# Latent attention layer on one core: the probabilities are split into halves before they are turned, and two transposing DMAs per query tile turn them in place of TensorE

## The reference, cut to what matters

```python
q_c = hidden @ Wq_c.T + bq_c                    # 192 latent channels
q   = (q_c @ Wq_up.T + bq_up)                   # 32 heads x (128 + 64)
kv  = hidden @ Wkv_c.T + bkv_c                  # 64 latent + 64 shared rope channels
k_nope, v = split(kv[:, :64] @ Wkv_up.T + bkv_up)    # 32 heads x (128 + 128)
scores = einsum('bhqd,bhkd->bhqk', q, [k_nope, k_rope]) / sqrt(192)
attn   = softmax(scores)                        # 1024 x 1024 for each head and batch
o      = einsum('bhqk,bhkv->bhqv', attn, v)
out    = o @ Wo.T summed over the heads + bo     # Wo is 512 x 128
```

## Time and profile before

| | |
|---|---|
| median of 3 runs | 1908.35 us (1903.71 to 1908.86) |
| the profiled execution's own time | 1908.44 us |
| its span (first to last instruction) | 1906.4 us |
| mean granted TensorE clock | 0.996 of full speed |
| busy: PE, DVE, ACT, POOL | 1878.7, 1615.1, 1398.4, 1237.8 us |
| the loop over the 128 rounds | about from 95 to 1800 us |
| one round in the middle | 13.2 us |

### The profile page before, as it was taken

How to read it: one execution, slowest core, us unless ns; L and a number is a source line. 1 busy time by engine, 2 the same in 40 slices (tenths; PEclk the granted TensorE clock), 3 DMA queues, 4 the chain that set the end, 5 groups by cost and what they waited for, 6 DMA issues and landing times. The chain is left out here.

```text
span 1906.4 us, 31285 instructions
## 1 busy us (share of the span) xinstructions
PE 1878.7 (99%) x11028; PEld 1174.0 (62%) x11028; DVE 1615.1 (85%) x2600; ACT 1398.4 (73%) x2491; POOL 1237.8 (65%) x1356
## 2 busy tenths in 40 slices
PE   7899999999999999999999999999999999999999
PEld 6756666665666666666666666666666666666544
DVE  5678888888888888888888888888888888888775
ACT  5567777777777777777777777777777777777622
POOL 3346766777666777777767667676666766767620
PEclk9999999999999999999999999999999999999999
DMA  5522112121111111111111111111112211111201
GB/s 205 175 83 45 42 38 45 35 45 38 41 43 36 45 35 45 46 34 45 40 40 42 38 45 36 43 45 34 45 35 45 46 34 45 37 43 41 84 33 58
DMA packets 74421, 96.68 MB, mean 51 GB/s; under 512 B 25856, under 2 KB 48416, under 8 KB 74272
## 3 DMA queue, kind: packets, MB, share of 16 engines
q1 hardware_dynamic: 70176, 86.33, 17.4%
q0 software_dynamic: 4096, 8.40, 1.3%
HBM read 83.95 MB, written 10.75 MB: 50 GB/s over the span
## 5 line engine op out<-in xcount | busy, mean ns | idle before, releaser
L965 DVE TENSOR_TENSOR PTL<-X,PTH 128x512 f16<-128x512 f32 x1024 | 657.1, 683 | 146.7 <-ACT PTH L913 146.3
L913 ACT ACTIVATE PTH<-X 128x512 f16<-128x512 f32 x1024 | 554.3, 594 | 236.0 <-PE X L815 236.0
L982 DVE TENSOR_REDUCE mx<-S 128x1 f32<-128x1024 f32 x512 | 621.4, 1214 | 3.0 <-PE S L838 3.0
L931 ACT ACTIVATE prob<-S,shift,unscale 128x1024 f32<-128x1024 f32 x512 | 620.3, 1212 | 0.3 <-DVE shift L988 0.2
L815 PE MATMUL X<-ident,prob 128*128 128x128 f32 x4096 | 538.0, 274 | 5.1 <-ACT prob L931 3.7
L815 PEld LDWEIGHTS X<-ident,prob 128*128 128x128 f32 x4096 | 458.3, 140 | 131.0 <-ACT prob L931 91.6
L836 PE MATMUL S<-kvTH,qeH 128*128 128x512 f16 x1024 | 388.1, 379 | 0.0
L837 PE MATMUL S<-kvTL,qeH 128*128 128x512 f16 x1024 | 388.1, 379 | 0.0
L838 PE MATMUL S<-kvTH,qeL 128*128 128x512 f16 x1024 | 388.1, 379 | 0.0
L777 POOL TENSOR_TENSOR onormH<-osum,recip_row 128x512 fp32r<-128x512 f32 x127 | 194.7, 1533 | 283.3 <-ACT osum L940 283.3
L843 PE MATMUL O<-PTH,kvn 128*128 128x512 f16 x1024 | 262.7, 379 | 0.6 <-DVE qef L971 0.4
(11 more groups left out here) (256 smaller groups left out, 2022.2 us busy)
## 6 DMA issues: line engine op xcount, KB each, us to landing
recip_row<-row_scratch SPq DMA_DIRECT2D x128, 256.0 KB, 4.3
weff<-weff_scratch SPq DMA_DIRECT2D x128, 192.0 KB, 4.5
wv<-in_wv POOLq DMA_DIRECT2D x128, 64.0 KB, 2.7
raw<-in_raw SPq DMA_DIRECT2D x8, 772.0 KB, 6.6
weff_scratch<-w_split SPq DMA_DIRECT2D x8, 768.0 KB, 5.8
x<-in_x SPq DMA_DIRECT2D x4, 1024.0 KB, 6.9
x_all<-in_x SPq DMA_DIRECT2D x3, 1024.0 KB, 5.8
out<-y SPq DMA_DIRECT2D x3, 1024.0 KB, 4.3
```

Source lines behind the costliest of these rows:

```text
L913: nc.scalar.activation(PTH[p][:, part:part + 4, unit * P:(unit + 1) * P], X[:, k % 2, :].rearrange("p (k c) -> p k c", k=4), ACT.Copy).the ...
L931: nc.scalar.activation(prob[u][:], S[:, u % 2, :], ACT.Exp, bias=shift[:, col:col + 1], scale=keep["unscale"][:, 0:1], accum_out=rs[:, col ...
L965: v.tensor_tensor(PTL[p][at], X[:, k % 2, :].rearrange("p (k c) -> p k c", k=4), PTH[p][at], ALU.subtract).then_inc(low_out, 1)
L982: v.reduce_max(mx[:, col:col + 1], S[:, u % 2, :], AX.X).then_inc(max_ready, 1)
```

## The change

The probabilities are no longer turned by TensorE. The exponential writes fp32 back into the slot of `S` that it read. ACT then copies that slot, 1024 columns in one instruction, to the fp16 high part (`halves[u][:, 0, :]`), and DVE subtracts it from the slot to get the low part (`halves[u][:, 1, :]`), both still with queries on the partitions. SP turns each of the two with one transposing DMA from SBUF to SBUF, 128 by 1024 fp16, into `PT` (eight 128 by 128 blocks of the high part, and eight of the low part): the one of the high part after `high_out`, the one of the low part after `low_out`. `X` is gone and `S` has three slots; a slot is free when `low` has read it.

What else moves: the values' matmuls of a head run two rounds later and not one, in one piece behind `scores(0)` (`values`). ACT's copy of `O` to `osum` and the first exponential of a round stand behind them. ACT and no longer DVE makes `qef`; POOL makes both `qeH` (a new fp16 copy) and `qeL` (`split_q`). POOL no longer writes the stacked tiles `onormLH` and `wvHL`, and PE adds a head's output with three matmuls in place of two (`output`), at the end of the round. DVE's copy of `V` moves to head 2.

```diff
-        prob = [sb(f"prob{i}", [P, SEQ]) for i in range(UN)]
-        PTH = [sb(f"PTH{i}", [P, KEYT, BLK], F16) for i in range(2)]
-        PTL = [sb(f"PTL{i}", [P, KEYT, BLK], F16) for i in range(2)]
+        halves = [sb(f"halves{i}", [P, 2, SEQ], F16) for i in range(UN)]
+        PT = [sb(f"PT{i}", [P, 2 * KEYT, BLK], F16) for i in range(2)]
...
-        S = ctx.enter_context(nc.psum_tensor("S", [P, 2, SEQ], F32))
-        X = ctx.enter_context(nc.psum_tensor("X", [P, 2, BLK], F32))
+        S = ctx.enter_context(nc.psum_tensor("S", [P, SLOTS, SEQ], F32))
         O = ctx.enter_context(nc.psum_tensor("O", [P, BLK], F32))
         V = ctx.enter_context(nc.psum_tensor("V", [P, BLK], F32))
...
+            def turn(g, u, par):
+
+                cols = slice(u * P, (u + 1) * P)
+                sp.wait_ge(high_out, UN * g + u + 1)
+                sp.dma_start(PT[par][:, 0:KEYT, cols], halves[u][:, 0, :], transpose=True).then_inc(turned_high[u], 16)
+                sp.wait_ge(low_out, UN * g + u + 1)
+                sp.dma_start(PT[par][:, KEYT:2 * KEYT, cols], halves[u][:, 1, :], transpose=True).then_inc(turned_low[u], 16)
+
             def body(g, b, h, par):
+                last = 1 - par
                 if exists(g + 2):
                     load(g + 2, dram["weff_h"][(h + 2) % NH], par)
                 if exists(g - 1):
 
-                    last = 1 - par
-
                     sp.wait_ge(recip_ready, g)
                     sp.dma_start(dram["row"][last].rearrange("(p u) -> p u", u=UN),
                                  recip[:, last * UN:(last + 1) * UN]).then_inc(recip_out, 16)
+                if exists(g):
+                    if g >= 2:
+                        sp.wait_ge(pv_done, g - 1)
+                    turn(g, 0, par)
+                if exists(g - 1):
                     sp.wait_ge(recip_out, 16 * g)
                     sp.dma_start(recip_row[last][:], dram["row"][last].partition_broadcast(P)).then_inc(row_in[last], 16)
+                if exists(g):
+                    for u in range(1, UN):
+                        turn(g, u, par)
...
-            def low_q(nxt, i):
+            def split_q(nxt, i):
                 pool.wait_ge(q_copied, nxt + 1)
+                nc.gpsimd.tensor_copy(qeH[i][:], qef[i][:]).then_inc(q_high, 1)
+                pool.wait_ge(q_high, nxt + 1)
                 nc.gpsimd.tensor_tensor(qeL[i][:], qef[i][:], qeH[i][:], ALU.subtract).then_inc(q_low, 1)
...
-                    nc.gpsimd.tensor_tensor(wvs[:], wv[i][:], unit[:], ALU.mult).then_inc(copied, 1)
-                    nc.gpsimd.tensor_tensor(wvHL[i][0:KVL, :], wv[i][0:KVL, :], unit[0:KVL, :], ALU.mult)
+                    nc.gpsimd.tensor_tensor(wvs[:], wv[i][0:KVL, :], unit[0:KVL, :], ALU.mult).then_inc(copied, 1)
                     pool.wait_ge(copied, 2 * g)
-                    nc.gpsimd.tensor_tensor(wvHL[i][KVL:P, :], wvs[KVL:P, :], f32(wvH[i][KVL:P, :]),
-                                            ALU.subtract).then_inc(wv_split, 1)
+                    nc.gpsimd.tensor_tensor(wvL[i][:], wvs[:], f32(wvH[i][0:KVL, :]), ALU.subtract).then_inc(wv_split, 1)
...
-                    nc.gpsimd.tensor_tensor(turned(onormH[:]), turned(osum[:]), row, ALU.mult).then_inc(onorm_high, 1)
-                    nc.gpsimd.tensor_tensor(turned(onorm[0:KVL, :]), turned(osum[0:KVL, :]), row[0:KVL],
-                                            ALU.mult).then_inc(onorm_high, 1)
-                    pool.wait_ge(onorm_high, 2 * g - 2)
-                    nc.gpsimd.tensor_tensor(turned(onormLH[KVL:P, :]), turned(osum[0:KVL, :]), row[0:KVL],
+                    nc.gpsimd.tensor_tensor(in_order(onormH[:]), in_order(osum[:]), row, ALU.mult).then_inc(onorm_high, 1)
+                    nc.gpsimd.tensor_tensor(in_order(onorm[:]), in_order(osum[0:KVL, :]), row[0:KVL],
                                             ALU.mult).then_inc(onorm_ready, 1)
+                    pool.wait_ge(onorm_high, g - 1)
                     pool.wait_ge(onorm_ready, g - 1)
-                    nc.gpsimd.tensor_tensor(onormLH[0:KVL, :], onorm[0:KVL, :], f32(onormH[0:KVL, :]),
-                                            ALU.subtract).then_inc(onorm_low, 1)
+                    nc.gpsimd.tensor_tensor(onormL[:], onorm[:], f32(onormH[0:KVL, :]), ALU.subtract).then_inc(onorm_low, 1)
...
-            def transposes(g, k, unit):
-
-                if event(g, k) > 2:
-                    pe.wait_ge(low_out, event(g, k) - 2)
-                for j in range(4):
-                    tile = 4 * (k % 2) + j
-                    last = nc.tensor.transpose(X[:, k % 2, j * P:(j + 1) * P], prob[unit][:, tile * P:(tile + 1) * P], ident[:])
-                last.then_inc(x_filled, 1)
...
-                    if 4 * g + u >= 2:
-                        pe.wait_ge(probs_ready, 4 * g + u - 1)
+                    if t >= SLOTS:
+                        pe.wait_ge(low_out, t - SLOTS + 1)
...
+                def values():
+
+                    if on:
+                        pe.wait_ge(q_copied, g + 1)
+                    for u in range(UN):
+                        pe.wait_ge(turned_high[u], 16 * (g - 1))
+                    for kt in range(KEYT):
+                        mm(O[:], keep["kvn"][:, batch * KEYT + kt, :], PT[par][:, kt, :], start=(kt == 0), stop=False)
+                    for u in range(UN):
+                        pe.wait_ge(turned_low[u], 16 * (g - 1))
                     for kt in range(KEYT):
                         half = slice(kt % 2 * KVL, (kt % 2 + 1) * KVL)
-                        ins = mm(O[half, :], keep["kvn"][:, batch * KEYT + kt, 0:KVL], PTL[1 - par][:, kt, :],
-                                 start=False, stop=(kt >= KEYT - 2))
-                    ins.then_inc(pv_done, 1)
+                        last = mm(O[half, :], keep["kvn"][:, batch * KEYT + kt, 0:KVL], PT[par][:, KEYT + kt, :],
+                                  start=False, stop=(kt >= KEYT - 2))
+                    last.then_inc(pv_done, 1)
+
+                def output():
+                    pe.wait_ge(wv_split, g - 1)
+                    pe.wait_ge(onorm_high, g - 1)
+                    pe.wait_ge(onorm_low, g - 1)
+                    mm(V[:], wvH[par][:], onormH[:], start=False, stop=False)
+                    mm(V[:], wvH[par][0:KVL, :], onormL[:], start=False, stop=False)
+                    mm(V[:], wvL[par][:], onormH[0:KVL, :], start=False, stop=h == (1 if on else 0)).then_inc(wv_done, 1)
...
+                if on:
+                    scores(0)
...
+                if exists(g - 2):
+                    values()
+                if on:
+                    scores(1)
+                    if exists(g + 1):
                         next_queries()
...
+                    scores(2)
+                    scores(3)
...
+                if exists(g - 2) and exists(g - 1):
+                    output()
...
-            def high_q(nxt, h, i):
+            def copy_q(nxt, h, i):
                 act.wait_ge(q_filled, nxt + 1)
+                if nxt >= 2:
+                    act.wait_ge(q_low, nxt - 1)
                 bias, factor = keep["beff"][:, h:h + 1], keep["qscale"][:, 0:1]
-                nc.scalar.activation(qeH[i][:], O[:], ACT.Identity, bias=bias, scale=factor).then_inc(q_high, 1)
+                nc.scalar.activation(qef[i][:], O[:], ACT.Identity, bias=bias, scale=factor).then_inc(q_copied, 1)
...
+                def exp(u):
+                    t, col = UN * g + u, par * UN + u
+                    act.wait_ge(shift_ready, t + 1)
+                    nc.scalar.activation(S[:, t % SLOTS, :], S[:, t % SLOTS, :], ACT.Exp, bias=shift[:, col:col + 1],
                                          scale=keep["unscale"][:, 0:1],
                                          accum_out=rs[:, col:col + 1]).then_inc(probs_ready, 1)
...
+                def high(u):
+                    t = UN * g + u
+                    act.wait_ge(probs_ready, t + 1)
+                    if g:
+                        act.wait_ge(turned_high[u], 16 * g)
+                    nc.scalar.activation(halves[u][:, 0, :], S[:, t % SLOTS, :], ACT.Copy).then_inc(high_out, 1)
+
+                if exists(g - 2):
+                    if g >= 3:
+                        act.wait_ge(onorm_high, g - 2)
+                        act.wait_ge(onorm_ready, g - 2)
+                    act.wait_ge(pv_done, g - 1)
+                    nc.scalar.activation(osum[:], O[:], ACT.Copy).then_inc(o_out, 1)
+                if exists(g):
+                    for u in range(UN):
+                        if u == 2 and exists(g + 1):
+                            copy_q(g + 1, (h + 1) % NH, 1 - par)
+                        exp(u)
+                        high(u)
...
+            def low(t):
+                u = t % UN
+                dve.wait_ge(high_out, t + 1)
+                if t >= UN:
+                    dve.wait_ge(turned_low[u], 16 * (t // UN))
```

(6 more changed lines are left out.)

216 lines of the change are left out of this document (73 added, 143 removed).

## The result

The changed kernel takes 2011.7 us (median of 4 runs, 2007.2 to 2014.6) against 1908.5 us: 1.0545 times the time, with a 95% interval of 1.0518 to 1.0571. It is 5.5% slower; 2080 us was forecast, 9%.

A forecast was written before the change was run, and what follows sets the result against it. SP's queue was taken to bound the round: 8 x (0.32 + 1.36) plus 1.07 for plain DMAs, 14.5 us. 1908.4 + 127 x (14.5 - 13.17) + 2 = 2080 us; 8-in-10 range 1845 to 2750.

The forecast's parts named there:

- What bounds before, and PE's work: PE sets the 13.17 us round; without transposes (4.20) and with a third output matmul (0.22) its work falls to 9.2 us.
- DVE and ACT by their work: Per round, DVE's work about 11.0 us plus 0.2, ACT's 11.1; neither engine binds above 11.3 us.
- The loop: Chain from one round's osum over qef, POOL and PE to the next: 12.7 us, bounds 12.4 and 13.1.
- The transposing DMAs: Eight per round on SP's queue, issue (0.32 us) and movement (1.36) following each other: a round of 14.5 us.
- the loop's case: Rival: DMAs are hidden and the osum-to-osum chain binds, 1853 us; chance 0.30, of which 0.26 faster.
- The ends: Before the loop nothing changes; behind it the last head's low part and turn add about 2 us.
- Short units: Rival: transposing DMAs move 32-byte units, 5.1 us each, a round of 44 us, 5900 us; chance 0.17 (above 2750 us).
- The clock's fall: Rival: PE idles before scores(0), its clock halves, scores and values double, round 16.9 us, 2385 us; chance 0.10.
- What was to be seen: Signs: SP's transposing DMAs 1.7 us apart without waits; PE in values and ACT waiting for DMAs; round 14 to 15 us.

The follow-up runs named there:

- experiment 3: Changed kernel with each low part's DMA turning only half of the keys, the rest of the low part left out of the output: 1925.9 us, ratio 1.0087.
- experiment 7: Changed kernel with one transposing DMA per tile (high and low parts together) and POOL scaling and splitting only an eighth of the output columns: 1953.1 us, ratio 1.0215.
- experiment 1: Kernel before the change, with unused transposing and plain DMAs issued on SP's otherwise empty queue in the feed-forward part: 1908.0 us.
- 9: Changed kernel with one transposing DMA per tile, osum copied behind the first tile's exponential, and half of the low part's keys turned: 1863.0 us, ratio 0.9779.
- 4: Changed kernel with one transposing DMA per tile, high and low parts together behind the low part, four per round: 1926.3 us, ratio 1.0088.
- 10: Changed kernel with both transposing DMAs of a tile waiting for its low part, the number of DMAs kept: 2012.4 us, ratio 1.0530.
- 8: Changed kernel with one transposing DMA per tile and osum copied behind the first tile's exponential: 1959.9 us, ratio 1.0259.

## Why the prediction was right in sign and too high

The forecast's sign was luck. Its sum got there by a time on SP that isn't so, and with the measured one it would have forecast a faster kernel. What made this one slower is no term of the sum.

**What bounds before, and PE's work.** Right that PE stops being the bound; its size was off. In the regular stretch it is busy for 82%, 10.7 us of a round of 13.1, where 9.2 were forecast. The rest, I take it, is the last matmul ahead of each wait, which is recorded with its full 0.38 us.

**DVE and ACT by their work.** Right within a few hundredths for the subtraction (1.216 against 1.25 us) and for the high part (1.02 against 1.08). Neither engine bound.

**The loop.** Forecast 12.7 us, with bounds 12.4 and 13.1; measured 13.08, and 12.5 with the later `osum`. POOL's new copy costs 0.61 us, not 0.95. What was missing is a stall of DVE by POOL. Three pairs of lines from the timeline after:

```profile
979.99 1.26 POOL L793 TENSOR_TENSOR onormL<-onorm,onormH 64x512 fp32r<-64x512 f32 x1
...
980.70 0.57 DVE L971 SCALAR_TENSOR_TENSOR shift<-mx,unscale,c_lift 128x1 f32<-128x1 f32 x1
...
986.18 0.22 DVE L971 SCALAR_TENSOR_TENSOR shift<-mx,unscale,c_lift 128x1 f32<-128x1 f32 x1
...
993.23 1.51 POOL L789 TENSOR_TENSOR onorm<-osum,recip_row 64x512 f32<-64x512 f32 x1
...
993.54 1.22 DVE L971 SCALAR_TENSOR_TENSOR shift<-mx,unscale,c_lift 128x1 f32<-128x1 f32 x1
...
996.77 1.15 POOL L759 TENSOR_TENSOR qeL<-qef,qeH 128x512 f16<-128x512 f32 x1
...
997.06 0.89 DVE L971 SCALAR_TENSOR_TENSOR shift<-mx,unscale,c_lift 128x1 f32<-128x1 f32 x1
```

The shift takes 0.22 us by itself (at 986.18). Beside POOL it ends within 0.02 us of POOL's end each time (981.27 and 981.25, 994.76 and 994.74, 997.95 and 997.92). In the regular round it meets POOL's output right behind `osum`, and the second tile's exponential waits for it; in experiment 3:

```profile
961.00 1.52 POOL L792 TENSOR_TENSOR onorm<-osum,recip_row 64x512 f32<-64x512 f32 x1
...
961.36 1.18 DVE L975 SCALAR_TENSOR_TENSOR shift<-mx,unscale,c_lift 128x1 f32<-128x1 f32 x1
...
962.58 1.18 ACT L922 ACTIVATE S<-S,shift,unscale 128x1024 f32<-128x1024 f32 x1 [0.95 <-DVE shift L975]
```

Those 0.95 us, less 0.34 for the copy and a little elsewhere, are the 0.4 us. The mean of the shift had 291 ns in the earlier trace rows, and has 498 after; the 291, above the 220 of a shift by itself, already held such meetings, for instance with `qeL`. Two things show that the stall lies in the loop: in experiment 7, where POOL's output work is an eighth, the shortest regular rounds are 12.1 us; and in the changed kernel's round from 682.4 us POOL's output starts 1.30 us behind `osum` and not 0.73, the shift before the second exponential takes 0.29 us, and the round lasts 12.2.

**The transposing DMAs: the step that failed.** "My value is that issue and movement follow each other on SP" is wrong. A DMA holds SP for 1.23 to 1.35 us, not for 0.32 + 1.36 = 1.68, and the movement lies beside the next issue (experiment 1). The prediction put the point from which the loop binds at 1.45 us of SP per DMA; with 1.34 on SP, its sum gives the loop's case, about 1850 us. That is the luck in the sign. The kernel is slower nevertheless, since the forecast took the longest of several resources as the round. It had 12.6 us for the engines' work, beside a loop of 12.7, and the sentence that a queue with no gap puts its delay somewhere stood only as an argument against a rival. It should have been a term of the sum. By estimate there are 12.8 us of DMA work in a loop of 13.08, and SP's queue is taken up for 12.3 us of the mean round of 13.96, all but its 1.7 us of waiting. A delay is then passed on to the row of reciprocals, to `qeL` and to PE. Experiments 3 and 9 show that less to move takes this away, 4 and 10 that fewer DMAs do. Since experiment 3 also eases SP (its DMAs take 1.32 us in the mean, where the changed kernel has 1.46), it doesn't part the engines from the queue cleanly. Such delays alone are 23 of the 92 us; PE's lowered clock behind them is 67. What begins a delay is shown in part (experiment 3, the `instruction` packets). Why runs of regular rounds end when they do, the traces do not tell.

On both disagreeing rules of the Trainium skill the runs now have rows. For its page "Advanced Engine Details and Errata", section X-Bar Transpose (TRN2), with 350 to 400 GB/s for transposing DMAs: 256 KB in 1.39 us of all engines is 189 GB/s, the full stretches moved 187 to 201, and several queued ones 285 for a microsecond; the measurement decides. For the estimate of 1.7 us on SP from "DMA: Bandwidth & Descriptors", section Why a DMA increments its semaphore by 16 and not by 1: SP was held for 1.23 to 1.34 us, and a DMA with half of the tiles held it for 1.27, so it doesn't go by tiles at these sizes. (The time that the prediction puts beside this estimate, 2430 us, is a slip: its own sum with 1.7 us per DMA, 8 x 1.7 + 1.07, gives 14.7 us per round and about 2105 us.)

**The ends.** +2 us forecast behind the loop; it was 0.6 there and 3.1 ahead of the first `osum`. Not foreseen were the three block ends, 13 us more than before. One of them, in the timeline after:

```profile
575.04 0.68 DVE L1018 COPY vsum<-V 128x512 f32<-128x512 f32 x1
...
575.77 1.12 PE L864 MATMUL V<-wo,vsum 128*128 128x512 f32 x2 [2.31 <-DVE vsum L1018]
...
579.31 1.23 DVE L965 TENSOR_REDUCE mx<-S 128x1 f32<-128x1024 f32 x1 [3.59 <-PE S L836]
```

PE waits for DVE's copy of `V`, projects, and only then gives DVE its next scores; DVE's maximum and with it ACT wait for 3.6 us. That the transposes filled such gaps before is argued, not tested.

**The rivals.** The loop binding is what the regular rounds do (ACT's line 934 waits for PE's line 851 in each), and experiment 9 shows it with a quarter less to turn. As a forecast for this kernel it was wrong. Short units are out: 1056 packets per DMA. The clock's fall happens, in 36 of 124 rounds. The rival had it in every round, at 4.2 us; here it costs 1.9 us in the mean where it happens. It had a part all the same, 67 of the 92 us. It needs a late `qeL` first, so it makes delays dearer and doesn't begin them.

**What was to be seen.** DMAs back to back, yes, but 1.38 us apart and not 1.7, with SP waiting 1.7 us per round. PE waiting in `values` for a DMA: line 851 did 10 times, 4.4 us; that sign was wrong.

## What to carry to other kernels

When an edit moves work from a full engine to the DMA engines, add up that work per round, and give the sum a margin against the round's dependent chain: here an estimated 12.8 us of transfers in a chain of 13.1 cost 0.7 us per round, and 10 us cost nothing. Of the 0.7 us more than 0.5 came through TensorE's lowered clock behind the delays: an edit that gives a full PE idle time in one gap has to count that too. Fewer and larger transposing DMAs paid in experiment 4, since each holds its queue for over 1.2 us at both sizes that were tried by themselves. A mean round hides all this; the list of single rounds, with each one's clock, tells a longer period from a period that breaks.

## What was not expected of the hardware

- A transposing DMA holds the issuing queue for 1.27 us with 128 x 512, 1.23 to 1.34 with 128 x 1024, and at least 1.34 with 128 x 2048 elements of 2 bytes. Plain ones of 128 x 1024 from SBUF to SBUF went out 0.61 us apart.
- Its packets are of 256 bytes, 1024 for 256 KB, also where the target is contiguous, and take 21 ns each on an engine when the DMA is alone. With several queued the engines moved 285 GB/s for a microsecond, where one alone moves 189.
- A 128 x 1 instruction of DVE that reads and writes only SBUF, started beside one of POOL's tensor-tensor instructions, lasts until that one's end, 1.22 us where it takes 0.22 alone (in experiment 3, 126 of the 126 that met `onorm`). In the last 0.15 us of `qeL` it isn't held (none of 122).
- The slowest transposing DMAs of experiment 3 stood, all 47, beside a packet of an `instruction` queue.
- A delay of about 1 us ahead of PE's gap cost another 1.9 us by the lowered clock (34 rounds).
- A shorter loop made the kernel slower, twice (experiments 7 and 8 against 4).
